# Other PSUM banks for values and up products, a transposed routed context, activations' low parts on GpSimd, and new instruction orders

## What is computed

```
h = LayerNorm(LayerNorm(patches(x)) @ W + b)                    # 196 x 768 -> 196 x 192
h = h + causal_attention(LayerNorm(h))                           # 12 heads, relative term in the keys
g = LayerNorm(h); n = LayerNorm(g)
s = sigmoid(n @ Wr + br); the 29 tokens of smallest s are "routed"
routed rows:  softmax(q k^T / 4) v @ Wo + bo                     # 12 heads, all 196 keys
other rows:   (n + s * weighted mean of n) @ Wm + bm
h2 = g + merged;  block = h2 + gelu(LayerNorm(h2) @ W1) @ W2     # 192 -> 768 -> 192
out = h + block
```

## Time and profile before

| | us |
|---|---|
| median of 3 runs | 5405.81 (5405.22 to 5406.14) |
| the profiled execution's own time | 5405.02 |
| its span, first to last instruction | 5403.3 |
| mean granted TensorE clock | 0.976 |

### The profile page before, as it was taken

One profiled execution on the slowest core, in us unless ns is written; L12 is line 12 of the kernel. 1 busy time (PEld: TensorE's weight loads), 2 busy tenths in 40 slices (PEclk: granted clock), 3 DMA queues, 4 the chain that ended last, 5 costly groups with the idle time before them and its releaser, 6 DMA issues.

```text
span 5403.3 us, 148048 instructions
## 1 busy us (share of the span) xinstructions
PE 4984.4 (92%) x47192; PEld 4747.0 (88%) x47192; DVE 4447.4 (82%) x13784; ACT 3768.9 (70%) x12542; POOL 2748.9 (51%) x3889
## 2 busy tenths in 40 slices
PE   3899999999999999999999999999999999999998
PEld 3898899889889989888988998898898899889887
DVE  3788888888888888888888888888888888888886
ACT  1677767767777776776777777677677777767765
POOL 2455555555555555555555545555555554545552
PEclk7999999999999999999999999999999999999998
DMA  4333333333333343333333324333333333323330
GB/s 65 43 39 40 48 39 38 48 40 39 44 44 39 40 48 39 38 47 41 39 43 45 39 38 50 39 38 47 41 39 43 45 39 38 49 39 39 46 42 6
DMA packets 297270, 224.89 MB, mean 42 GB/s; under 512 B 38604, under 2 KB 296985, under 8 KB 297241
## 3 DMA queue, kind: packets, MB, share of 16 engines
q1 hardware_dynamic: 284990, 221.88, 32.8%
q10 hardware_dynamic: 12251, 2.65, 0.3%
HBM read 205.18 MB, written 19.27 MB: 42 GB/s over the span
## 4 chain that ended last, share of the span: by engine, by line
issue 47%; POOL 30%; POOLq 18%; PE 2%; DVE 1%; ACTq 1%; ACT 0%; DVEq 0%; DMA 0%
POOL p L519 15%; POOL rstd L501 3%; POOLq L537 3%; POOLq L526 3%; POOLq L572 2%; POOL h2b L573 2%; POOL h1b L511 2%; POOLq L500 2%; POOL y_row L568 2%; POOLq L531 2%; POOLq L569 2%; POOL sqsum L540 2%; POOL rstd L582 2%; POOL rstdf L584 1%; POOLq L539 1%
## 5 line engine op out<-in xcount | busy, mean ns | idle before, releaser
L519 POOL TENSOR_TENSOR p<-p,rden 98x392 f32<-98x392 f32 x1152 | 949.9, 845 | 952.6 <-DVE rden L1232 952.6
L1597 ACT ACTIVATE p<-banks,negmax 98x98 f32<-98x98 f32 (+1 forms) x3072 | 1142.2, 381 | 187.7 <-DVE negmax L1216 98.7
L1216 DVE TENSOR_REDUCE negmax<-banks 98x2 f32<-98x392 f32 (+1 forms) x1152 | 629.4, 556 | 74.8 <-PE banks L712 59.8
L712 PE MATMUL banks<-kz,qk_parts 128*98 128x392 f32 x2304 | 664.1, 384 | 0.0
L1597 ACT ACTIVATION_READ_ACCUMULATOR p<-banks,negmax 98x1 f32 x3072 | 616.2, 201 | 0.0
L723 PE MATMUL banks<-tokw,x_sb 128*98 128x193 f32 x3072 | 573.5, 336 | 15.5 <-POOLq L531 15.5
L723 PEld LDWEIGHTS banks<-tokw,x_sb 128*98 128x98 f32 x3072 | 545.1, 254 | 18.4 <-issue 15.5
L664 PE MATMUL banks<-z3Ts,w_split 128*128 128x196 f32 x3840 | 519.8, 282 | 1.4 <-DVE z3Ts L1187 1.4
L954 PE MATMUL banks<-w,gparts 128*98 128x192 f32 x4608 | 515.8, 269 | 0.2 <-DVE gparts L1410 0.2
L747 PE MATMUL banks<-ident,p 98*98 98x98 f32 x4608 | 487.7, 250 | 4.2 <-ACTq L1601 4.2
L954 PEld LDWEIGHTS banks<-w,gparts 128*98 128x98 f32 x4608 | 477.3, 176 | 3.7 <-issue 0.3
(11 more groups left out here) (277 smaller groups left out, 13265.8 us busy)
## 6 DMA issues: line engine op xcount, KB each, us to landing
x_sb<-in_x SPq DMA_DIRECT2D x384, 196.0 KB, 4.8
x_sb<-in_x SPq DMA_DIRECT2D x256, 190.8 KB, 8.4
x_sb<-in_x SPq DMA_DIRECT2D x256, 185.5 KB, 10.4
x_sb<-in_x SPq DMA_DIRECT2D x128, 189.0 KB, 6.9
out<-out_row SPq DMA_DIRECT2D x128, 147.0 KB
pT<-in_L_ffn_W ACTq DMA_DIRECT2D x1, 576.0 KB
gstore<-in_L_ffn_W SPq DMA_DIRECT2D x1, 384.0 KB
gstore<-in_L_ffn_W ACTq DMA_DIRECT2D x2, 192.0 KB
```

Of the source, the lines that this page charges most:

```text
L519: gp.tensor_tensor(heads, heads, rden[:, g, t, s0:s0 + sn].unsqueeze(2).broadcast_to([HT, sn, w]), ALU.mult).then_inc(sem["pnorm_sb"], 1)
L712: last = mm(o, qparts[:, g, HT * t:HT * t + HT], kz[:, part, slots[0]:slots[-1] + 1, g, 0:w], start=False, stop=part == 1, skip_group_chec ...
L1216: ve.tensor_reduce(negmax[:, g, t, slots[0]:slots[-1] + 1], bank[RING[f"S{k}"]][0:HT, 0:w * len(slots)].rearrange("p (s w) -> p s w", w=w) ...
L1597: sc.activation((p1 if t else p0)[0:HT, 4 * g + s], bank[b][0:HT, w * i:w * i + w], ACT.Exp, bias=negmax[:, g, t, s:s + 1], accum_out=den[ ...
```

## The change

`values` writes bank 6 and up(0), up(1), up(2) write banks 7, 6, 6; the waits follow (values waits for the last GELU, the first embedding product and up(1) wait for values' copy, up(2) waits for the second GELU, and down(0) no longer waits for it by itself). `context2` computes the routed context transposed, with the values as the stationary side (64 columns) and the probabilities moving (128 columns), two groups into the two halves of the partitions; `context2_cols` and its two products are gone on PE, and DVE instead adds the bias and masks the heads in two operations and sums the four heads' blocks in two more. POOL scales the routed probabilities by their inverse sums before they are transposed (new wait pn2_sb on PE), and makes the low parts of the three GELU results (`gelu_low`), which DVE made before; DVE still rounds the high part. Nothing in the functions that make the keys changes, only their place among the calls. All four engines get new orders.

```diff
                     gp.tensor_tensor(h1b[:], h1[:], both(bp), ALU.add).then_inc(sem["h1b_sb"], 1)
 
+                def gelu_low(j):
+
+                    gp.wait_ge(sem["gphi_sb"], after("gphi_sb", k, j + 1))
+                    at = slice(2 * j, 2 * j + 2)
+                    gp.tensor_tensor(gparts[:, 1, at], gT[:, j % 2], gparts[:, 0, at].bitcast(F32),
+                                     ALU.subtract).then_inc(sem["gparts_sb"], 1)
+
...
+                if back:
+                    gp.wait_ge(sem["rden2_sb"], after("rden2_sb", m))
+                    gp.tensor_tensor(probs2[:], probs2[:],
+                                     rden2[:].unsqueeze(2).broadcast_to([128, NG, T]),
+                                     ALU.mult).then_inc(sem["pn2_sb"], 1)
...
                 def values():
                     if again:
-                        pe.wait_ge(sem["out_sb"], all_before("out_sb", k))
+                        pe.wait_ge(sem["gelu_sb"], all_before("gelu_sb", k))
                     pe.wait_ge(sem["aTs_sb"], after("aTs_sb", n))
-                    cols_to_rows(7, aT, split["wv"], "v_mm")
+                    cols_to_rows(6, aT, split["wv"], "v_mm")
...
+                        if front:
+                            pe.wait_ge(sem["v_sb"], after("v_sb", n))
                         pe.wait_ge(sem["xlast_sb"], after("xlast_sb", l))
                     last = patches(TOK_BANK, t, q0, q1)
...
                 def transposes2():
-                    pe.wait_ge(sem["probs2"], after("probs2", m))
+                    pe.wait_ge(sem["pn2_sb"], after("pn2_sb", m))
                     for t in range(2):
...
                 def context2():
                     pe.wait_ge(sem["p2T_sb"], after("p2T_sb", m))
-                    for g in range(NG):
+                    for groups in ((0, 1), (2,)):
                         for t in range(2):
-                            last = mm(bank[4][:, 64 * g:64 * g + 64],
-                                      p2T[:, t, 128 * g:128 * g + 128],
-                                      vv[:, t, 64 * g:64 * g + 64], start=t == 0, stop=t == 1)
+                            for g in groups:
+                                part, at = 64 * (g % 2), 128 * (g // 2)
+                                last = mm(bank[4][part:part + 64, at:at + 128],
+                                          vv[:, t, 64 * g:64 * g + 64],
+                                          p2T[:, t, 128 * g:128 * g + 128], start=t == 0,
+                                          stop=t == 1, skip_group_check=True)
                     last.then_inc(sem["ctx_mm"], 1)
...
-                def context2_cols():
-                    pe.wait_ge(sem["ctx_sb"], after("ctx_sb", m))
-                    mm(bank[5][:, 0:SELP], ctxm[:, 0:2], stack32[:], start=True, stop=True)
-                    last = mm(bank[5][0:64, SELP:2 * SELP], ctxm[:, 2], stack32[:], start=True,
-                              stop=True)
-                    last.then_inc(sem["ctxT_mm"], 1)
 
...
-                    if front:
-                        pe.wait_ge(sem["v_sb"], after("v_sb", n))
                     rows_to_cols(7, z3, "z3_T")
 
                 def up(j):
 
                     if j == 0:
                         pe.wait_ge(sem["z3Ts_sb"], after("z3Ts_sb", k))
+                    if j == 1:
+                        if front:
+                            pe.wait_ge(sem["v_sb"], after("v_sb", n))
                         if head:
                             pe.wait_ge(sem["tok_y"], after("tok_y", l))
                     if j == 2:
-                        pe.wait_ge(sem["gelu_sb"], after("gelu_sb", k, 1))
+                        pe.wait_ge(sem["gelu_sb"], after("gelu_sb", k, 2))
                     for f in (2 * j, 2 * j + 1):
-                        last = cols_to_cols(bank[(6, 7, 6)[j]][:, T * (f % 2):T * (f % 2) + T],
+                        last = cols_to_cols(bank[(7, 6, 6)[j]][:, T * (f % 2):T * (f % 2) + T],
                                             z3Ts, split["w1"], 128 * f, 128 * f + 128)
                     last.then_inc(sem["up_mm"], 1)
 
                 def down(j):
 
-                    if j == 0:
-                        pe.wait_ge(sem["gelu_sb"], after("gelu_sb", k, 2))
                     pe.wait_ge(sem["gparts_sb"], after("gparts_sb", k, j + 1))
                     for f in (2 * j, 2 * j + 1):
...
+                def inverse2():
+                    ve.wait_ge(sem["probs2"], after("probs2", m))
+                    ve.reciprocal(rden2[:], den2[:]).then_inc(sem["rden2_sb"], 1)
+
                 def context2():
-                    ve.wait_ge(sem["probs2"], after("probs2", m))
-                    ve.reciprocal(rden2[:], den2[:])
-                    ve.drain()
+
                     ve.wait_ge(sem["ctx_mm"], after("ctx_mm", m))
-                    for g in range(NG):
-                        last = ve.scalar_tensor_tensor(
-                            ctxm[:, g], bank[4][:, 64 * g:64 * g + 64], rden2[:, g:g + 1],
-                            diag_of[:].rearrange("p h e -> p (h e)"), ALU.mult, ALU.mult)
-                    last.then_inc(sem["ctx_sb"], 1)
-
-                def context2_cols():
-                    ve.wait_ge(sem["ctxT_mm"], after("ctxT_mm", m))
                     for chunk, (lo, hi) in enumerate(KC):
                         size = hi - lo
-                        last = ve.tensor_scalar(ctxT[0:size, chunk, 0:SELP],
-                                                bank[5][0:size, SELP * chunk:SELP * (chunk + 1)],
-                                                fbv[0:size, chunk:chunk + 1], None, ALU.add)
+                        ve.scalar_tensor_tensor(
+                            ctxm[0:size, chunk].rearrange("p (h i) -> p h i", i=SELP),
+                            bank[4][0:size, 128 * chunk:128 * chunk + 128].rearrange(
+                                "p (h i) -> p h i", i=SELP), fbv[0:size, chunk:chunk + 1],
+                            head_of[0:size].unsqueeze(2).broadcast_to([size, 4, SELP]), ALU.add,
+                            ALU.mult)
+                    ve.drain()
+                    for chunk, (lo, hi) in enumerate(KC):
+                        size = hi - lo
+                        last = ve.tensor_reduce(
+                            ctxT[0:size, chunk, 0:SELP],
+                            ctxm[0:size, chunk].rearrange("p (h i) -> p i h", i=SELP), AX.X,
+                            ALU.add)
                     last.then_inc(sem["ctxT_sb"], 1)
...
                     at = slice(2 * j, 2 * j + 2)
-                    ve.tensor_copy(gparts[:, 0, at], gT[:, j % 2])
-                    ve.drain()
-                    ve.tensor_tensor(gparts[:, 1, at], gT[:, j % 2], gparts[:, 0, at].bitcast(F32),
-                                     ALU.subtract).then_inc(sem["gparts_sb"], 1)
+                    ve.tensor_copy(gparts[:, 0, at], gT[:, j % 2]).then_inc(sem["gphi_sb"], 1)
```

More of the change, by code:

```diff
@@ L556, in step @@
                     normalised(5)
+                if front:
+                    h1_with_bias()
+                if head:
+                    gp.wait_ge(sem["tok_var"], after("tok_var", l))
+                    rstd(var1[:], ve1[:], rstd1[:], "tok_rstd")
+                if back:
+                    gp.wait_ge(sem["rden2_sb"], after("rden2_sb", m))
[3 more added lines that the diff above has]
+                if front:
+                    normalised(6)
                 if head:
@@ L570, in step @@
                     gp.tensor_tensor(h1[:], y_row[:], both(ln2b), ALU.add).then_inc(sem["h1_sb"], 1)
-                if back:
-                    gp.drain()
-                    gp.tensor_tensor(h2b[:], h2[:], both(bf2), ALU.add).then_inc(sem["h2b_sb"], 1)
+                if tail:
+                    gelu_low(0)
                 if head:
@@ L576, in step @@
                     rstd(mv_a[:, :, 1], ve3[:], rstd3[:], "h1_rstd")
+                if tail:
+                    gelu_low(1)
+                if tail:
+                    gelu_low(2)
                 if front:
@@ L968, in step @@
                     keys()
-                    values()
-                    queries()
-                if head:
-                    embed(0,0,QX)
                 if back:
-                    keys2()
                     score()
@@ L977, in step @@
                     mlp_cols()
+                if back:
+                    keys2()
+                    values2()
+                if front:
+                    queries()
+                if back:
+                    gather()
+                    mixing_rows()
                 if front:
@@ L980, in step @@
                     causal("S1")
-                if back:
-                    values2()
-                if front:
                     causal("S2")
-                if back:
-                    mixing_rows()
+                    causal("S3")
                 if head:
-                    square_sums()
-                if front:
```

(43 more changed lines are left out.)

123 lines of the change are left out of this document (57 added, 66 removed).

## The result

The changed kernel takes 5286.5 us (median, 5285.9 to 5288.5) against 5406.0 for the kernel before: a ratio of 0.978, 95% interval 0.976 to 0.980. It is 119 us faster. Forecast were 309 us less, a time of 5096 us. The time lies in the range, near the 5296 that rival 1 gave, but the gain is less than half of the forecast. The profiled execution of the changed kernel has a span of 5284.2 us.

The account below looks back on a forecast made before the run. PE was taken to bound the kernel, with DVE close behind. PE's order of 36.5 us plus waits and seam gave 38.5 us a step against 40.97; over 125 steps 309 us less, 5096 us, range 5000 to 5310.

Parts of the forecast that it names:

- rival 1: DVE becomes the bound: 3.1 us of waits remain, 5296 us with clock falls, 5234 without; chance 0.22.
- What bounds, and the clock: PE sets the end; clock falls after the projection's wait in one step in three, costing 0.51 us a step.
- (d): Projection: up(2) after attention covers the chain through L1391, so the wait of 1.57 us goes whole.
- (a): First scores (S0): PE waits 0.5 us for the chain from the keys; the old 0.3 at L648 goes.
- (b): up(0): PE waits 0.55 us for patch variance and z3's low parts; 0.95 at the routed transposes goes.
- (c): attn_out: PE waits 0.5 us for DVE's chain from the low parts through the routed context.
- The walk (part 3): Laying the four engines' new orders against each other gives 38.2 us a step, 38.5 with the seam of two steps.
- what DVE and POOL do to each other: Single-input SBUF operations of DVE wait for a running POOL instruction; charged at y_row and the seam.
- rival 4: DVE-POOL sharing stalls eleven roundings and normalisations; 3.0 us more on the chain, 41.5 us a step, 5471 us; chance 0.09.
- Part 2: Work changing engine: DVE falls from 34.5 to some 33 us a step, POOL rises from 21.4 to 25.7.
- Part 1: PE's own work: context2 from 1.32 to 0.86 us, context2_cols gone (0.45); own order 37.4 to 36.5 us.

Follow-up runs that it names:

- b3: Kernel before with only two calls turned round (attention ahead of attention_input on VectorE, of gelu(2) on ScalarE): 5275.6 us, ratio 0.976.
- e5: Changed kernel with TensorE's up(2) behind the projection instead of ahead of it: 5487.9 us, ratio 1.015.
- e4: Changed kernel with the GELU low parts back on VectorE, new orders, banks and transposed context kept: 5410.9 us, ratio 1.001.
- e9: Changed kernel with only mlp_cols_lo (low parts of z3) moved into VectorE's wait for the routed scores: 5207.1 us, ratio 0.963.
- e6: Changed kernel with GpSimd's two bias additions early, after a wait for the selection, and inverse_sums(3) behind q_blocks: 5160.8 us, ratio 0.955.
- e1: Changed kernel with GpSimd's h2 and h1 bias additions moved right behind the patch fix-up: 5324.0 us, ratio 0.985.
- e2: Changed kernel with VectorE's inverse_sums(3) moved behind q_blocks: 5294.2 us, ratio 0.980.
- b1: Kernel before with only the GELU low parts moved to GpSimd: 5822.5 us, executions from 5693.6 to 5829.3.

## Why the prediction was wrong

**What bounds, and the clock: right.** PE sets the end, the projection's wait brought the clock down (b3, which shortens it, has no low clock in the steady part either), and it is gone: 0.51 of 0.51 us a step.

**(d), the projection: right.** The wait went whole; e5 shows the cover, e4 that it needs the low parts out of DVE's way, b3 that nearly half of it was to be had by turning two calls round.

**(a), (b), (c): right in place and about in size.** Each was counted with 0.2 of tail: (a) 0.22 + 0.2 against 0.5; (b) 0.34 + 0.2 against 0.55, and e9 removes it; (c) 0.21 + 0.2 against 0.5. The routed transposes wait for nothing.

**The walk (part 3) and the paragraph on what DVE and POOL do to each other: wrong, and here the time went.** The step that failed is the walk's: it has no wait before the routed scores, where PE waits 0.72 + 0.2. The stalls of the operations ahead of them, L1333 and L1347, were put at nothing. The term that was mis-sized is the stalls: three were charged, all of operations with a single input. In the step there are besides them L1347, L1323 and L1333, and in the experiments L1253 and L1288, which read two SBUF tensors. The page of the Trainium skill that I cited names this kind too (GPSIMD Engine Reference, Specifications: contention with VectorE instructions in a two-port mode "or with two SBUF inputs"), and I did not charge it. The trace agrees: L1347, with two inputs, went from 276 to 924 ns. L1333 and L1347 lie ahead of the routed scores with 0.94 us of stall between them, and when both are gone (e6) the wait is gone. a_row, 1.37 us beside a subtraction, holds attention_cols up by 0.24: `scatter` ahead of it takes 0.60 from its start to the next where it took 0.36 before, and a_row ends at 2668.28.

```profile
2666.91 1.37 DVE L1180 TENSOR_SCALAR a_row<-h,mv_a,rstd 98x192 f32<-98x192 f32 x2
```

```profile
2667.74 0.52 PE L901 MATMUL banks<-ao,selT 128*98 128x192 f32 x4
2668.34 0.56 PE L665 MATMUL banks<-ident,a_row 98*128 98x98 f32 x4
```

It was rival 4's mechanism, which I put at 0.09 and priced at 3.0 us of stalls on the chain; about 1.2 us came, and most of it from operations that are not among the eleven of that rival.

**Part 2: wrong for DVE, right for POOL.** The forecast took DVE from 34.5 to 33 us; it went to 35.7, with 2.7 us of stalls that it did not have before. POOL's new work came as priced: 1.03 us for a subtraction, 1.17 against 1.25 for the scaling, 26.3 us a step against 25.7. But the forecast looked for the danger in this new work, and e4 shows that about 2.0 of the 2.7 us come without the subtractions.

**Part 1: half right.** context2's twelve records take 1.02 us of order instead of 0.86, against 1.32 before. Products into two halves of the partitions do overlap, as forecast: taken one by one, the two records of a pair start 7 ns apart, and one pair follows the other after 0.109 us, as one record follows the other where they run alone. So four products' worth of slots was right; the 0.16 more lies at the ends (0.16 us for the first pair, 0.20 from the last record to PE's next). context2_cols is gone.

```profile
2659.90 1.09 PE L870 MATMUL banks<-scratch,vv 98*64 98x128 f32 x12
2660.92 1.55 PE L764 MATMUL banks<-ident,p 98*98 98x98 f32 x16
```

But PE's own order did not fall from 37.4 to 36.5: 40.0 less 2.9 us of waiting (the 1.66 of the rows, 0.2 of tail for each of five, and 0.24 for a_row) is 37.1. Of these 0.6 us 0.16 is context2's. Some 0.3 shows where PE starts again after a wait: attn_out takes 0.71 from start to next start against 0.51 in the kernel before, the first scores 0.43 against 0.33. Where the rest arises is open.

So the missing 1.5 us a step are 0.9 before the routed scores, 0.24 before attention_cols and 0.6 in PE's own order, less some 0.2 by which the forecast's own waits came out shorter. e6 gives the first back, and a little more, by taking the stalls away; the other two stay for the most part.

**Rival 1's 5296 is near the measured time by luck.** It had 3.1 us of waits, and 2.9 came, but it got to its time with a clock that falls in every third step, which did not happen, and with an own order of 36.5 where 37.1 was measured. Without falls it gave 5234.

## What to carry to other kernels

A cost in an engine's own table is not enough when work moves to GpSimd, and as little when only the order changes: list what VectorE operations with all their inputs in SBUF will run beside each GpSimd instruction, and what stands behind them. Here about three quarters of the stalls came without the work that moved (e4). Put GpSimd's work beside VectorE operations that read PSUM (e6: 126 us for moving two additions and one reciprocal). After each move look at which operation now is the long one of its form, since a stall tends to reappear at the next (e1, e2). And before a large change, try the two calls that stand ahead of the longest wait: here they alone gave as much as the whole change.

## What the runs showed of the hardware

- A stalled VectorE operation ended with the GpSimd operation beside it or shortly behind, however small it was: a product of 98 by 2 numbers took 0.99 us instead of 0.16 and ended 0.02 behind (e2), L1347 0.14 behind, two halves of a_row took 2.32 us beside 1.98 us of subtraction (b1). It goes both ways: POOL's L525 took 1.40 instead of 0.84 while DVE's L1344, which began after it, ran its normal 0.41.
- Products into the two halves of the output partitions, 64 columns each, ran beside each other: 0.109 us from pair to pair as from one to the next alone, with 128 moving columns (changed kernel, L870).
- TensorE's granted clock: with a wait of 0.78 (b3) or of 1.03 and 0.80 us in the step (e5) it stayed at 2.4 GHz through the steady part; with 1.37 us (the kernel before) it fell to 1.2 GHz in one step of three; with 2.49 us in each step of b1's profiled execution. The kernels differ in what PE does around the wait too, so this is no threshold. But the price of a wait is not its length: the 0.59 us that b3 took from it were worth 1.04 us a step, since the lost clock went with them.
